# Relu of the edge messages and the comparison of the score pass, written as operations of two tensors, in a graph network on one core

## The reference

```python
score = jnp.einsum('ehd,ehd->eh', q[dst], k[src]) * rel_pri / SQRT_DK     # attention
...
ea = jax.nn.silu(edge_attr @ We + be)                                     # once
for l in range(L):                                                        # L = 4
    msg = jax.nn.relu(x[src] + ea)
    agg = jax.ops.segment_sum(msg, dst, num_segments=n)
    h = x + agg
    h = jax.nn.silu(h @ W1[l] + b1[l]) @ W2[l] + b2[l]
    y = x + h
    x = (y - mu) * jax.lax.rsqrt(var + LN_EPS) * gamma[l] + beta[l]
```

## Time and profile before

| | |
|---|---|
| median of 3 runs | 9549.08 us (9542.76 to 9550.45) |
| profiled execution | 9545.06 us, span from first to last instruction 9543.3 us |
| busy: POOL, PE, DVE, ACT | 6696.7 (70%), 4661.5 (49%), 4305.5 (45%), 529.1 us (6%) |
| score pass | about 232 to 1316 us |
| attention sum with its scans | 1316 to 2055 us |
| four edge layers | 2055 to 6484 us |
| convolutions and linear aggregation | 6484 to 9543 us |

### The profile page before, as it was taken

How to read it: one execution, slowest core, us unless ns; L and a number is a source line. 1 busy time by engine, 2 the same in 40 slices (tenths; PEclk the granted TensorE clock), 3 DMA queues, 4 the chain that set the end, 5 groups by cost and what they waited for, 6 DMA issues and landing times.

```text
span 9543.3 us, 143586 instructions
## 1 busy us (share of the span) xinstructions
PE 4661.5 (49%) x19975; PEld 3800.2 (40%) x19976; DVE 4305.5 (45%) x9490; ACT 529.1 (6%) x1108; POOL 6696.7 (70%) x6591
## 2 busy tenths in 40 slices
PE   2766735544455344544445444453455444544455
PEld 1444424433344333433334333343444334443444
DVE  3455565654566445654456445672223223332222
ACT  1222211100000000000000000000000000000000
POOL 1777626557777677767777677776777677767776
PEclk9577768865566556565556555665555555555566
DMA  3998854223333333333333333331222222222222
GB/s 102 262 271 263 249 153 128 83 77 98 99 101 101 88 98 102 100 89 98 98 100 101 87 97 99 99 90 45 54 54 57 51 53 56 55 51 53 54 58 53
DMA packets 907432, 960.76 MB, mean 101 GB/s; under 512 B 442719, under 2 KB 610042, under 8 KB 906872
## 3 DMA queue, kind: packets, MB, share of 16 engines
q0 software_dynamic: 213248, 462.82, 18.9%
q1 hardware_dynamic: 572380, 399.74, 15.4%
q10 hardware_dynamic: 121756, 97.77, 3.1%
HBM read 801.39 MB, written 164.71 MB: 101 GB/s over the span
## 4 chain that ended last, share of the span: by engine, by line
POOL 55%; issue 21%; DMA 9%; DVE 6%; PE 4%; DVEq 2%; POOLq 1%; ACTq 1%; SPq 1%; ACT 0%
POOL rows L693 52%; DMA gates_by_edge<-gate 7%; PE ps_seg L823 2%; POOL msg L713 1%; POOL sums L693 1%; POOLq L324 1%; DVE msg L1452 1%; PE ps_mm L847 1%; DMA rows<-node_rows,idx 0%; DMA kv_rows<-gate 0%; PE ps_big L878 0%; PE ps_t L835 0%; ACTq L368 0%; DVE group_stats L1355 0%; DVEq L1288 0%
## 5 line engine op out<-in xcount | busy, mean ns | idle before, releaser
L693 POOL DMA_INDIRECT rows<-node_rows,idx x5488 | 5573.0, 1015 | 1919.1 <-issue 1669.6
L823 PE MATMUL ps_seg<-msg,onehot 128*128 128x128 f32 (+1 forms) x9800 | 2142.0, 387 | 2553.1 <-DVE sums L1309 2274.6
L823 PEld LDWEIGHTS ps_seg<-msg,onehot 128*128 128x128 f32 x9800 | 1838.0, 279 | 2854.2 <-DVE sums L1309 2535.0
L1288 DVE SCALAR_TENSOR_TENSOR onehot<-iota_f,win_base,dst_ch 128x512 f32<-128x512 f32 x1968 | 1512.9, 769 | 3200.4 <-PE ps_seg L823 2554.6
L823 PE MATMUL ps_seg<-rows,onehot 128*128 x5880 | 1393.7, 417 | 1559.9 <-SPq L590 1450.7
L823 PEld LDWEIGHTS ps_seg<-rows,onehot 128*128 128x128 f32 x5880 | 1220.9, 310 | 1729.8 <-issue 1728.2
L1452 DVE TENSOR_TENSOR msg<-q_res,rows 128x512 f32 (+1 forms) x984 | 677.1, 688 | 1108.8 <-SPq L590 1108.7
L693 POOL DMA_INDIRECT sums<-kv_rows,idx x784 | 773.4, 987 | 288.2 <-issue 230.0
L713 POOL TENSOR_TENSOR msg<-rows,score 128x512 f32 x245 | 325.4, 1330 | 420.6 <-SPq L590 197.0
L1309 DVE TENSOR_TENSOR sums<-sums,ps_seg 128x128 f32 (+1 forms) x1952 | 550.9, 282 | 0.1
L796 PE MATMUL ps_mm<-w_edge,attr_t 65*128 65x512 f32 x488 | 377.8, 867 | 195.0 <-ACT attr_t L949 191.0
(11 more groups left out here) (189 smaller groups left out, 1923.8 us busy)
## 6 DMA issues: line engine op xcount, KB each, us to landing
q_res<-gates_by_edge SPq DMA_DIRECT2D x784, 256.0 KB
rows<-node_rows,idx POOLq DMA_INDIRECT x5488
gates_by_edge<-gate ACTq DMA_DIRECT2D x244, 256.0 KB
rows<-dst_padded SPq DMA_DIRECT2D x196, 256.0 KB, 4.9
value_rows_by_edge<-sums SPq DMA_DIRECT2D x196, 256.0 KB
rows<-value_rows_by_edge SPq DMA_DIRECT2D x196, 256.0 KB, 2.6
idx<-src_padded SPq DMA_DIRECT2D x1568, 2.0 KB
node_rows<-h_res ACTq DMA_DIRECT2D x49, 448.0 KB
```

Of the source, the lines that this page charges most:

```text
L693: pool.indirect_dma_start(target[:, r, j, :], None, table, bass.IndirectOffsetOnAxis(ap=idx[:, r, j:j + 1], axis=0)).then_inc(rows_landed[ ...
L823: last = nc.tensor.matmul(ps_seg[u][:, 0:width], onehot[:, u, j, :], rhs(j), start=j == 0, stop=j == J - 1)
L1288: V.scalar_tensor_tensor(onehot[:, u, :, :], iota_f[:, :].rearrange("p (a n) -> p a n", a=1).to_broadcast([P, J, P]), win_base[:, ds(w, 1) ...
```

## The change

Two DVE operations, each of which had one tensor and one scalar operand, get a second tensor operand in the scalar's place. It is a view with step zero of a column that is there already: `zero_col`, cleared at the start, for the Relu (maximum with 0.0), and the column of `node_id` for the comparison. The operators, the outputs, the waits and the semaphores stay.

```diff
             def mark_nodes(s, u, c, slot, w):
 
                 dve.wait_ge(dst_row_ready, c + 1)
-                V.tensor_scalar(onehot_t[:, u, :, :].rearrange("p j e -> p e j"),
+                V.tensor_tensor(onehot_t[:, u, :, :].rearrange("p j e -> p e j"),
                                 dst_rows[:, ds(slot, 1), :].rearrange("p s (e j) -> p (s e) j", j=J),
-                                node_id[:, ds(w, 1)], None, ALU.is_equal).then_inc(onehot_ready, 1)
+                                node_id[:, ds(w, 1)].rearrange("p (a b) -> p a b", a=1).to_broadcast([P, P, J]),
+                                ALU.is_equal).then_inc(onehot_ready, 1)
...
+            zeros_as_msg = zero_col[:, :].rearrange("p (a b) -> p a b", a=1).to_broadcast([P, J, D])
+
             with dve.Fori(0, LAYERS) as l:
...
                     dve.wait_ge(gates_added, l * N_ONEHOT + s + 1)
-                    V.tensor_scalar(msg[:, u, :, 0:D], msg[:, u, :, 0:D], 0.0, None, ALU.max).then_inc(msg_ready, 1)
+                    V.tensor_tensor(msg[:, u, :, 0:D], msg[:, u, :, 0:D], zeros_as_msg, ALU.max).then_inc(msg_ready, 1)
```

## The result

The changed kernel takes 9569.88 us (median of ten runs, 9562.34 to 9576.89), the kernel before 9547.56 (ten runs, 9542.76 to 9556.71): ratio 1.0023, 95% interval 1.0014 to 1.0033, so 22 us or 0.2% **slower**. The forecast was 9513, 36 us faster. The range (9460 to 9640) holds the time, the sign is wrong. The profiled execution after took 9568.94 us with a span of 9567.1, against 9545.06 and 9543.3.

A forecast was written before the change was run, and what follows sets the result against it. POOL's gathers, some held by DVE operations, were taken as the bound. Layers -63 us plus score pass +27 gave -36: profiled 9545.06 to 9509, median 9549 to 9513. Range 9460 to 9640.

The forecast's parts named there:

- the rhythm of the forecast: Back-to-back layer steps: two gathers per step, one free, one held by the Relu, losing 66 ns instead of 430.
- What bounds the kernel: POOL's indirect gathers and the issue time between them, 98% of the chain through the first layer pass.
- the rule of the holds: A running two-tensor DVE operation holds a gather about 0.13 us into its work; 0.817 us remain after DVE lets go.
- Rival B: New operations hold no gathers: POOL gains 129 us in the runs, -100 in total, 9449 us; chance 0.06.
- The Relu's price: Two-tensor Relu at L1456 takes 688 ns, +0.261 us per DVE step; the repeated operand costs nothing extra.
- Steps of 2303 + 261 = 2564 ns: Back-to-back DVE steps in the layers lengthen by the Relu's full 261 ns, which changes the gather pattern.
- the 129 us of gain: POOL time saved in back-to-back layer steps: 364 ns in each of 354 steps.
- Three gathers take two steps: Old pattern in back-to-back layer steps, with gathers held by L1288 and L1452, losing 430 ns per step.
- 26 per pass less 5.5 at the end: First three layer passes: 0.94 of POOL's 26 us gain, less 5.5 for longer end Relus, 19 us earlier each.
- 3 x 5.5 + 13: Layer-pass ends: 21 longer Relus cost 5.5 us in three passes; in the fourth, 76 cost 19.8 against 6.5 of waiting.
- 1221: Score pass comparison L1212 takes 1221 ns, 688 plus 533 for strided writes, bounds 688 and 1221; +27 us together.
- Rival C: Rhythm doesn't unlock, longer holds count in full elsewhere: +94 us, 9643; mean layer gather above 1032 ns; chance 0.16.

The follow-up runs named there:

- relu_only: Kernel before with only the Relu made a two-tensor operation, old comparison kept; 11319.34 us, ratio 1.0062.
- compare_only: Kernel before with only the comparison made a two-tensor operation, old Relu kept; 11258.93 us, ratio 1.0004.
- both_again: The changed kernel itself, both operations two-tensor, run again beside its parts against the kernel before; 11470.29 us, ratio 1.0047.
- relu_only_2: Second run of the kernel before with only the Relu made two-tensor, old comparison kept; 11513.31 us, ratio 1.0046.
- compare_only_2: Second run of the kernel before with only the comparison made two-tensor, old Relu kept; 11458.35 us, ratio 1.0010.

## What the forecast step rests on: who makes the idle time

**PE's sum shortened.** `three_matmuls_before` and `three_matmuls_after` leave out the last of the four products of each sum (one of a partition's four edges).

```diff
-                for j in range(J):
-                    last = nc.tensor.matmul(ps_seg[u][:, 0:width], onehot[:, u, j, :], rhs(j), start=j == 0, stop=j == J - 1)
+                terms = J if isinstance(k, int) and k == 1 else J - 1
+                for j in range(terms):
+                    last = nc.tensor.matmul(ps_seg[u][:, 0:width], onehot[:, u, j, :], rhs(j), start=j == 0, stop=j == terms - 1)
```

> The kernel before with three of the four matmuls of a step's sum in the layer and convolution passes (a quarter of the edges is left out of the sums, so the output is not the reference's). Theory 1 (the run of steps is a loop of two steps through PE: sum 2.08 us, 0.46 till the one-hot starts, 2.01 till the addition ends, 0.05; half of 4.60 is the period 2.30): with a sum of about 1.56 the period of back-to-back steps falls towards VectorE's own length, 2.05 to 2.10 us, and the 0.26 us before L1288 all but vanish. Rival (those 0.26 are VectorE's own issue time, as the prediction took them): the period stays 2.30.

> The changed kernel with three of the four matmuls of a step's sum in the layer and convolution passes (a quarter of the edges is left out). Theory 1: the period falls from 2.37 only to VectorE's own length, 2.28 to 2.32 us, which is 0.23 to 0.26 above the same edit of the kernel before: with PE out of the loop the Relu's full lengthening shows, as the prediction had it. Rival: the difference between the two stays 0.06 us, as with four matmuls.

They took 11413.77 and 11425.67 us (one run each, the kernel before 11460.26 beside them), with a quarter of the edges missing from the sums. Their use is the step, not the time. Take each two consecutive steps in which neither addition of messages waits, and halve the distance. These periods don't spread, they fall on levels:

| | steps | levels, us (count) |
|---|---|---|
| before | 168 | 2.23 to 2.25 (40), 2.32 to 2.35 (102), 2.37 (17) |
| after | 172 | 2.24 to 2.26 (14), 2.32 to 2.35 (22), 2.43 to 2.45 (114) |
| three_matmuls_before | 188 | 2.23 to 2.25 (106), 2.32 to 2.35 (59) |
| three_matmuls_after | 200 | 2.24 to 2.26 (111), 2.32 to 2.35 (54) |

With the long sum the Relu moves most steps from 2.33 to 2.435. With the short one it moves them from 2.235 to 2.245, and the level of 2.435 is gone. Both expectations missed: the shortest periods were to be 2.05 to 2.10 and 2.28 to 2.32, 0.23 to 0.26 apart, and they are 2.235 and 2.245. With PE's sum out of the way the Relu's full length still doesn't show. So there are two waits, one behind the other.

The first is a loop of two steps with PE. A one-hot buffer is free again when PE's sum of two steps before has ended. For the earlier trace rows, in the kernel before:

```profile
3008.11 2.07 PE L823 MATMUL ps_seg<-msg,onehot 128*128 128x128 f32 x8 [0.23 <-DVE sums L1309]
...
3012.40 0.27 DVE L1309 TENSOR_TENSOR sums<-sums,ps_seg 128x128 f32 x1
...
3012.73 1.16 PE L823 MATMUL ps_seg<-msg,onehot 128*128 128x128 f32 x8 [0.29 <-DVE sums L1309]
```

And L1288's register instructions there, from 3009.7 to 3010.7 (duration in ns, starts):

```profile
L1288 DVEq ALU_OP  x3: 40/53/53, 3010.2 to 3010.5; - x3
L1288 DVEq FUSED_REGOPS  x2: 53/55/57, 3010.4 to 3010.6; - x2
```

PE's sum ends at 3010.18. The first of the five register instructions, which carries the wait for that sum, starts at 3010.23, and the five fill the time up to the one-hot at 3010.66, 0.48 after PE's end. From there to the end of L1309 it is 2.01, and PE starts its next sum 0.06 later: 2.07 + 0.48 + 2.01 + 0.06 = 4.62 for two steps, 2.31 per step. The Relu's 0.27 is in this loop once, that is half per step: 4.89, 2.44 per step. That is the 4.89 of the stretch after, and the level of 2.435.

The second is in DVE's own stream. The rows of three_matmuls_after:

```profile
3577.57 0.75 DVE L1290 SCALAR_TENSOR_TENSOR onehot<-iota_f,win_base,dst_ch 128x512 f32<-128x512 f32 x1
3578.23 0.69 DVE L1456 TENSOR_TENSOR msg<-q_res,rows 128x512 f32 x1
3578.95 0.69 DVE L1460 TENSOR_TENSOR msg<-msg,zero_col 128x512 f32<-128x512 f32 x1
3579.56 0.28 DVE L1311 TENSOR_TENSOR sums<-sums,ps_seg 128x128 f32 x1
3579.87 0.75 DVE L1290 SCALAR_TENSOR_TENSOR onehot<-iota_f,win_base,dst_ch 128x512 f32<-128x512 f32 x1
...
3581.86 0.28 DVE L1311 TENSOR_TENSOR sums<-sums,ps_seg 128x128 f32 x1
3582.06 0.75 DVE L1290 SCALAR_TENSOR_TENSOR onehot<-iota_f,win_base,dst_ch 128x512 f32<-128x512 f32 x1
```

From start to start the shortest steps of the kernel before have 669 ns (one-hot to addition), 719 (to the Relu), 343 (to L1309) and 437 (to the next one-hot), 2167 in all, with 0.157 us idle at the end; those after have 669, 719, 609 and 198, 2187 as measured from addition to addition (the 198 as from 3581.86 to 3582.06 above; the 0.31 us of 3579.56 to 3579.87 belongs to the steps of 2.30). The Relu grew by 266 and what follows it shrank by 239. From the Relu's start to the next one-hot's it is 780 ns before and 807 after, though DVE worked only 0.43 and 0.28 us of the 780. The records of DVE's queue show what fills it. From the Relu's start to the next one-hot the queue works through eight or ten register instructions, depending on the step. With PE's sum shortened they follow one another without a wait for it, and they set the step: with eight of them it takes 2.167 us before and 2.194 after, with ten 2.302 in both. The longer Relu runs beside them. The level of 2.24 is a pair of an eight and a ten; the level of 2.33 that stays with the short sum is the mean of 2.30 and of 2.36, a ten with some instructions of another kind that take longer.

The wait for PE can be counted in the same records. Of the back-to-back steps of the layers the register instruction in front of the one-hot was kept waiting for PE's sum by 0.04 us or more in 145 of 383 before and in 187 of 389 after, and in none of some 350 in each kernel with the short sum.

**The length or the form.** `relu_half` has the two-tensor Relu on two of the four edges of a partition, so that it has the new form and the old length; the old comparison is kept. It ran on the chip where the kernel before takes 9548.13.

```diff
-                    V.tensor_tensor(msg[:, u, :, 0:D], msg[:, u, :, 0:D], zeros_as_msg, ALU.max).then_inc(msg_ready, 1)
+                    V.tensor_tensor(msg[:, u, 0:J // 2, 0:D], msg[:, u, 0:J // 2, 0:D], zeros_as_msg, ALU.max).then_inc(msg_ready, 1)
```

> The kernel before with the two-tensor Relu over half of the elements only (two of a partition's four edges; the messages of the others go unrectified into the sums). It has relu_only's form and the old Relu's length: some 0.43 us, 343 ns from its start to the start of the next operation. If the length of DVE's step is what relu_only costs, the ratio is that of compare_only or less, 0.9985 to 1.0010, and the back-to-back periods are 2.235 and 2.33 us as before. If it is the form (the operand, its way to memory, what the instruction takes to be fetched), the ratio stays at 1.004 to 1.006 whatever the length.

```profile
L1458 DVE TENSOR_TENSOR msg<-msg,zero_col x984: 426/427/502, 2073.2 to 6453.8; 128x256 f32<-128x256 f32 x197
...
DVE onehot L1288 <- issue: 609.1, 957, 4.8
```

It took 9547.84 us, ratio 1.0000 (0.9991 to 1.0009). The Relu has 427 ns, the idle places before the one-hot are back (957), the levels are those of before (37 steps at 2.23 to 2.25, 109 at 2.32 to 2.35). So the form costs nothing here, and what the Relu does, it does by its length. (The messages of the other two edges go into the sums without a Relu.)

**More length.** `scalar_relu_twice` is the kernel before with its Relu done twice, the second waiting for the first. It ran beside relu_half.

```diff
+                    V.tensor_scalar(msg[:, u, :, 0:D], msg[:, u, :, 0:D], 0.0, None, ALU.max).then_inc(relu_done, 1)
+                    dve.wait_ge(relu_done, l * N_ONEHOT + s + 1)
                     V.tensor_scalar(msg[:, u, :, 0:D], msg[:, u, :, 0:D], 0.0, None, ALU.max).then_inc(msg_ready, 1)
```

> The kernel before with its Relu, of a tensor and a scalar, done twice, the second waiting for the first (the result is the same). The first takes some 460 ns from start to start with that wait, the second 343, so DVE's step is 0.46 us longer than before: between the changed kernel (0.27) and relu_twice (0.99, counting its wait). If the length of the step acts through the gathers' rhythm, as a curve that rises first and falls later (changed kernel 1.0047, relu_twice 0.9995), this lies on it, 1.001 to 1.006, with a period of 2.55 to 2.65 us. If relu_twice is quicker because of the added instruction and wait in DVE's stream, not because of length, the ratio is 0.994 to 0.999, as far below the kernel before as relu_twice is below the changed one.

It took 9594.84 us, ratio 1.0049 (1.0035 to 1.0063), 47 more. The time is in the expected range, but the period is longer than the 2.55 to 2.65 that I expected, 2.75 to 2.80 (idle times of 0.13 to 0.28 before the one-hot stay). With that the rhythm of the forecast does come. The gathers of the layer passes, relu_half first, then scalar_relu_twice:

```profile
2063.00:3124.00 1061.00, 820.83 (x784) 0.57 0.38 100
3162.00:4223.00 1061.00, 820.75 (x784) 0.57 0.38 100
4261.00:5324.00 1063.00, 823.19 (x784) 0.57 0.38 100
5362.00:6434.00 1072.00, 832.87 (x784) 0.58 0.37 99
```

```profile
2058.00:3109.00 1051.00, 805.16 (x784) 0.52 0.38 101
3165.00:4217.00 1052.00, 806.51 (x784) 0.52 0.38 101
4274.00:5324.00 1050.00, 804.32 (x784) 0.52 0.38 101
5380.00:6466.00 1086.00, 805.20 (x784) 0.52 0.37 98
```

POOL spends 76 us less in its gathers (3221.2 against 3297.6), most of it outside the back-to-back steps. And yet the kernel is slower. The ends of passes show where it went; first relu_half, then scalar_relu_twice, POOL's last gather of the first layer and the last addition after it:

```profile
3122.36 0.94 POOL L693 DMA_INDIRECT rows<-node_rows,idx  x1 [0.30 <-issue]
...
3134.44 0.69 DVE L1454 TENSOR_TENSOR msg<-q_res,rows 128x512 f32 x1
```

```profile
3107.19 0.94 POOL L694 DMA_INDIRECT rows<-node_rows,idx  x1 [0.30 <-issue]
...
3136.96 0.69 DVE L1453 TENSOR_TENSOR msg<-q_res,rows 128x512 f32 x1
```

The passes begin at 2063.79 and 2058.09. Measured from there the last gather starts 9 us earlier (1049.1 against 1058.6) and the last addition 8 us later (1078.9 against 1070.7): DVE has ten steps to do after it instead of five, in 29.8 us instead of 12.1. It is so far behind that 93 steps before the end no addition waits for rows any more; in relu_half and before these are 20. In sums over the four passes: held gathers -76, POOL's waits for a slot +60 (6 in each of three passes, 42 in the last), ends of passes +65 (237.5 against 172.5), +49 together, and the medians differ by 47. What POOL gains is more than lost again at the ends, since DVE is what ends a pass, and in waits for slots.

After the change itself it is the small form of this: from the last gather's start to the last addition 13.5, 13.3, 13.5 and 24.5 us against 12.1, 12.1, 12.1 and 20.5, +8 in all, which is the +7.4 of the table of ends.

**A Relu twice as long, in the other regime.** `relu_twice` is the changed kernel with the same doubling, beside both_again.

> The changed kernel with its Relu done a second time (the result is the same), so that DVE has another 609 ns from start to start in each of 984 steps. Theory 1: in back-to-back steps one-hot, addition, Relu, Relu and L1310 start 669, 719, 609, 609 and some 198 ns after one another, so the period is 2.80 us with no idle time before the one-hot, and the two-step loop with PE (2.08 + 0.46 + 2.86 + 0.05 = 5.45, 2.73 a step) no longer shows: the first 0.26 us cost 0.1 us a step there, the next 0.61 cost 0.37. Against the changed kernel of the same chip some 2 to 4 times what the changed Relu alone cost: 100 to 250 us. Rival (DVE has as much slack left as before, what costs is something else): period below 2.6 us, and less than 60 us.

It took 11407.79 us, ratio 0.9995 (0.9986 to 1.0004), 62 us less than both_again on the same chip, with a period of 3.01 to 3.07. That is a miss, in sign. Each layer pass is 13 to 25 us shorter from its first gather to its last. In the first of them POOL's waits of over 1 us fell from 271 to 192 us, while what held gathers lose rose from 58 to 111. The one-hot's idle times of over 3.5 us in the layers fell from 181 to 92. Why DVE's longer steps make the pauses of that regime fewer is left open.

## The sources of the holds, and of the comparison's length

**Operands in PSUM.** `relu_psum_zero` is relu_only with the column of zeros in PSUM; `iota_psum` is the kernel before with the one-hot's row of numbers in PSUM in all passes but the last. Both move the first product of the node updates to another bank for it.

```diff
 iota_psum
+            chain(V.tensor_copy(ps_big[1][:, 0:P], iota_f[:, :]))
...
-                                       iota_f[:, :].rearrange("p (a n) -> p a n", a=1).to_broadcast([P, J, P]),
+                                       numbers.rearrange("p (a n) -> p a n", a=1).to_broadcast([P, J, P]),
```

> The Relu as a two-tensor operation whose zero is read from PSUM, so that it has one source in SBUF; to free a PSUM bank the first product of the group update goes to the banks of the transposes. It should take 690 ns as in the changed kernel, but hold no gather (L1309, with a PSUM source, holds none). Theory 1 (what the longer Relu costs is its hold on the gathers, 40 us of POOL in the changed kernel, and the ends of the passes): the Relu's holds vanish, POOL's loss in the layers falls from 342 to about 300 us, the whole is 15 to 35 us below relu_only, ratio to before 0.997 to 0.9995. Rival (its length on VectorE is what costs, the holds are made up elsewhere by the phases): ratio 1.001 as relu_only.

> The kernel before, with one source of the one-hot L1288 (the numbers 0 to 127) in a PSUM bank in all passes but the last; the first product of the group update goes to the banks of the transposes. Theory 1 (an operation of VectorE holds a gather only if it reads two SBUF tensors, or runs on one at two elements a cycle): L1288 no longer holds any gather. Of the layers' 342 us of holds the one-hot's 197 go (some come back at L1452), and of the first two convolutions' 16 and 23 us nearly all: 120 to 200 us less, ratio 0.979 to 0.988. Rival (holds come from any running operation that reads SBUF): nothing changes, ratio 1.000.

> The same edit as relu_psum_zero (Relu of two tensors, its zeros read from PSUM), for a chip on which the kernel before runs near 9548 us. If a two-tensor Relu holds gathers only because both operands lie in SBUF, no gather ends 0.817 us after a Relu, and the layers' excess falls from some 86 to 60 to 78 us per pass, as the gathers that the Relu held meet L1288 or the addition instead; against relu_only_2 the time falls by 10 to 60 us, against the kernel before it lies at 0.995 to 1.001. If the holds were not what a layer pass waits for, the time is that of relu_only_2 plus some 10 us for slower access to PSUM.

> The same edit as iota_psum (kernel before, the one-hot's numbers read from PSUM in all passes but the last), for a chip on which the kernel before runs near 9548 us. If the holds of gathers set the time of the layers, those by the one-hot (197 us in four layers, 30 to 40 in two convolutions) vanish, the additions take over a part, the layers' excess falls from 86 to 30 to 50 us a pass, and the time falls by 120 to 240 us, ratio 0.975 to 0.988. If DVE and PE in their loop are next to late, the slots make POOL wait instead (57 ns more per step on DVE, some 25 us in all passes), and less than 60 us are gained. If the chip runs the kernel before near 11300 us, ratio 1.008 again.

| | median us | ratio, 95% interval |
|---|---|---|
| relu_psum_zero | 11349.21 | 1.0093, 1.0072 to 1.0114 |
| relu_psum_zero_2 | 11524.47 | 1.0065, 1.0049 to 1.0081 |
| iota_psum | 11337.52 | 1.0086, 1.0067 to 1.0106 |
| iota_psum_2 | 11518.79 | 1.0052, 1.0037 to 1.0067 |

The first two expectations missed. relu_psum_zero was to take the time of relu_only or less and takes 30 us more; iota_psum was to take the time of the kernel before or less and takes 87 us more. relu_psum_zero_2 takes 11 us more than relu_only_2, as its second case had it; iota_psum_2 was expected at 1.008. These chips can't show the gain that was forecast for the other regime.

The gathers of iota_psum_2 in the second layer and the first convolution, and then those of compare_only_2, whose one-hot is the old one:

```profile
3627.00:4944.00 1317.00, 763.14 (x784) 0.58 0.30 81
7810.00:9004.00 1194.00, 743.70 (x784) 0.58 0.18 46
```

```profile
3653.00:4941.00 1288.00, 799.91 (x784) 0.55 0.31 82
7736.00:8920.00 1184.00, 772.28 (x784) 0.58 0.19 46
```

784 gathers of 944 ns are 740.1 us. With the one-hot's numbers in PSUM the convolution's gathers lose 4 us to holds instead of 32, the layer's 23 instead of 60. And of relu_psum_zero, where 263 gathers started under a Relu that would hold them (225 in the second run), none ends 0.82 us behind one; in relu_only 223 do (211 in relu_only_2). So one operand in PSUM is enough, and the operation holds nothing. And the time rises all the same: these chips wait for DVE and PE, and the shortest step grew from 2.23 to 2.285 us. What this kernel does where POOL is the bound was not measured; there the four layers lose 197 us to L1288.

**The comparison's output.** `compare_straight_scalar` and `compare_straight_two` write the comparison in the order of the edges instead of transposed, in the old and the new form, on the kernel before; the one-hot is then laid out wrongly, so only the duration is of use.

```diff
-                V.tensor_scalar(onehot_t[:, u, :, :].rearrange("p j e -> p e j"),
-                                dst_rows[:, ds(slot, 1), :].rearrange("p s (e j) -> p (s e) j", j=J),
+                V.tensor_scalar(onehot_t[:, u, :, :],
+                                dst_rows[:, ds(slot, 1), :].rearrange("p s (j e) -> p (s j) e", j=J),
```

> The kernel before with L1212 reading and writing straight on (the one-hot is laid out wrongly, so the output is not the reference's). Theory 1 (the strided output costs the scalar form one cycle more per pair): 488 ns. Rival (the scalar form of this line runs one element a cycle): 753 ns as before.

> The kernel before with L1212 as an operation of two tensors that reads and writes straight on (the one-hot is laid out wrongly). Theory 1 (the 1036 ns of the changed kernel hold a cost of the strided output, 0.67 of a cycle per element): 690 ns. Rival (the repeated operand is what costs, as its pattern changes with every element of four): 1036 ns stays.

```profile
L1212 DVE TENSOR_SCALAR onehot<-rows,node_id x246: 485/486/726, 235.8 to 1559.2; 128x512 f32 x122, 128x512 f32<-128x512 f32 x1
```

```profile
L1212 DVE TENSOR_TENSOR onehot<-rows,node_id x246: 691/693/766, 235.4 to 1575.8; 128x512 f32 x122, 128x512 f32<-128x512 f32 x1
```

486 and 693 (11455.39 and 11427.90 us as wholes, one run each). The step of 512 bytes costs the scalar form 753 - 486 = 267 ns and the two-tensor form 1036 - 693 = 343 ns, 0.67 ns for each of 512 elements, where I had 533.

## Why the prediction was wrong

- **What bounds the kernel, and the rule of the holds: right.** Held gathers end 0.81 to 0.82 us after the operation that held them, the new Relu's too (3024.30 and 3025.12 above). In the layers of the trace after, 308 gathers end so behind a Relu and lose 40.5 us; before, 20 and 3.4. Rival B, that the new form holds nothing, falls with it. The Trainium skill, "SBUF — State Buffer", section "Who interferes with whom", infers that a two-tensor operation doesn't stall descriptor generation; by that inference rival B would hold, and the rows above speak against it once more. The section's own rule does fit: that an operation with two SBUF inputs contends with a GpSimd instruction that reads SBUF, and one with at most one SBUF input, outside the two-port modes, doesn't. The gathers read their indices from SBUF, and with one operand in PSUM none of 263 was held.
- **The Relu's price: right** (692 ns for 688), and that its repeated operand costs nothing (relu_half).
- **"Steps of 2303 + 261 = 2564 ns": the step that failed.** I added the Relu to the period as if DVE worked all through it. But its four operations take 0.67 + 0.72 + 0.34 + 0.28 = 2.01 us to the end of L1309, and the earlier trace rows itself shows the rest: 0.31 us idle before L1288, "issue". In that time DVE's queue waited for PE's sum and worked through register instructions, and most of the Relu's extra went into it. The period measured is 2.36 to 2.39 in the mean, 0.06 to 0.09 more and not 0.26. So the 129 us of gain never came: the sum of the holds is 342 us in both traces, with more gathers held (42% against 35%), each for less.
- **"Three gathers take two steps", 430 ns lost per step: mis-sized too.** I read a steady pattern from one group. Before the last gather of a pass the runs are one to three steps long, never longer (83, 35 and 59 of them). Sharing out each gather's time from start to start, they hold 1.60 gathers per step and lose 307 ns per step, 101 us together, so 129 could not be gained there. After the change it is 1.66 gathers and 295 ns.
- **The rhythm: right where a step is long enough.** scalar_relu_twice, at 2.76 to 2.80, has 2.01 gathers a step and loses 270 ns in each, near the 283 that a step of 2781 less two gathers of 1249 leaves. But its 76 us less of holds come mostly from the other steps; why is open.
- **"26 per pass less 5.5 at the end": the second error,** hidden by the first. The ends were counted as 21 steps, each longer by the Relu. A DVE that gets behind adds steps to the end: ten after the last gather instead of five. scalar_relu_twice had the gain and paid 65 us at the ends and 60 in waits for slots. So even with its rhythm the forecast would probably have been too low; no run has that rhythm with a step only 0.26 us longer.
- **Ends of passes at the small dose:** forecast 3 x 5.5 + 13, measured +7.4 in all; the last five steps of a pass grew by 0.05 to 0.1 each, not 0.26.
- **The comparison: 1036, not 1221.** The Trainium skill, "SBUF — State Buffer", section "Door 1: The DMA port swizzle", says that an access to a new line each time pays a penalty; the runs agree that there is one, 343 ns here, two thirds of what I took. The holds of the score pass rose by 42 us (forecast 36, from the longer operation), and POOL's wait for slots there fell from 57.0 to 28.9; the pass ended 13 us later, where 27 were forecast. Two thirds of the holds were absorbed, not four tenths. The 13 is not sharp: relu_half, with the old comparison, ended its score pass 8 us later than the trace before.
- **Rival C** had the right outcome (the rhythm doesn't unlock), for a reason of its own (scatter of the step lengths) and with the wrong price: 94 us. It let the longer Relu count in full elsewhere and at the ends. Its own test stands: the mean layer gather was to decide, 1019 for the forecast, above 1032 slower than before; it is 1053.

## What to carry to other kernels

Before adding time to an engine's step, look at the idle time inside that step: here an "issue" of 0.2 to 0.3 us in a run of back-to-back steps was a loop with another engine and the engine's own register instructions, and it swallowed most of the addition. Write down the loop, with its length in steps, and see which of its members the change touches. And when an engine off the bound gets slower, count not only its longer steps at the end of a stage but how many more of them will be left there.

## What was not expected of the hardware

- A three-operand operation with one of its tensors in PSUM holds no gather (4 us of holds in a convolution pass, 32 with all in SBUF); the price is 0.05 us a step.
- The periods of back-to-back steps lie on levels (2.235, 2.33, 2.435), within 0.03 us each, on all four chips. They come from the number of register instructions in DVE's queue (eight or ten behind the Relu, some 0.08 us apart) and from the loop with PE. A Relu of 692 instead of 427 ns beside ten of them costs nothing, beside eight 0.027 us.
- On three of the four chips the same program takes 18 to 20% longer. There register instructions of DVE often start 0.7 us apart, up to 1.4, and POOL waits for slots some fifty or sixty times a pass. What is fast or slow there is another question than on the fourth: 0.27 us more on DVE's step cost 55 to 68 us, and some 0.7 us on top of it cost less than none.
- Writing each element 512 bytes after the one before costs 267 ns in 512 elements for the form with a scalar and 343 for the form with two tensors.
